# First forward gate of the Mamba block stored raw and passed through silu between the directions

## The reference

```python
x = x + _L0_conv_ref(_gn(x), Wq, Wk, Wv)       # attention, 102 highest scores of 1024 kept per row
t = _to_tokens(x)
t = t + _L1_attn_ref(_ln_t(t), ...)            # Mamba in both directions
t = t + _L1_ffn_ref(_ln_t(t), ...)             # 8 experts, top 2
...
def _mamba(x, in_proj_w, conv_w, conv_b, x_proj_w, dt_proj_w, dt_proj_b, A_log, Dvec, out_proj_w):
    xz = x @ in_proj_w.T
    xs, z = jnp.split(xz, 2, axis=-1)
    ...
    xs = jax.nn.silu(xs)
    dbc = xs @ x_proj_w.T
    dt = jax.nn.softplus(dbc[..., :DT_RANK] @ dt_proj_w.T + dt_proj_b)
    ...
    _, hs = jax.lax.associative_scan(combine, (dA, dBu), axis=1)
    y = jnp.einsum('blds,bls->bld', hs, Cm) + xs * Dvec
    y = y * jax.nn.silu(z)
    return y @ out_proj_w.T
```

## Time and profile before

| | us |
|---|---|
| median of 3 runs | 1493.72 |
| the runs | 1494.01, 1493.72, 1484.97 |
| the profiled execution, its own time | 1495.54 |
| its span, first to last instruction | 1493.7 |
| TensorE busy | 1262.7 (85%) |
| VectorE busy | 1200.8 (80%) |
| ScalarE busy | 898.4 (60%) |
| GpSimd busy | 836.4 (56%) |
| mean granted TensorE clock | 0.937 |

### The profile page before, as it was taken

One profiled execution on the slowest core, in us unless ns is written; L12 is line 12 of the kernel. 1 busy time (PEld: TensorE's weight loads), 2 busy tenths in 40 slices (PEclk: granted clock), 3 DMA queues, 4 the chain that ended last, 5 costly groups with the idle time before them and its releaser, 6 DMA issues. The chain is left out here.

```text
span 1493.7 us, 17449 instructions
## 1 busy us (share of the span) xinstructions
PE 1262.7 (85%) x4573; PEld 641.1 (43%) x4573; DVE 1200.8 (80%) x1388; ACT 898.4 (60%) x1247; POOL 836.4 (56%) x450
## 2 busy tenths in 40 slices
PE   3609888898998988988888989889898998888868
PEld 1307344344546434433444634434354733434343
DVE  2695799998796689999688679999779479999920
ACT  1626766766555766767464676676574676676612
POOL 3022388788152378778235258878517238878815
PEclk8859899999989889999999979999999988999979
DMA  2000112222030112222021012222103011322203
GB/s 77 14 0 2 46 71 84 85 92 77 16 113 15 31 57 86 85 86 97 17 77 66 4 58 79 91 85 86 56 1 114 16 37 65 98 85 84 85 1 127
DMA packets 30506, 92.00 MB, mean 62 GB/s; under 512 B 4790, under 2 KB 8764, under 8 KB 30428
## 3 DMA queue, kind: packets, MB, share of 16 engines
q1 hardware_dynamic: 30428, 91.10, 18.0%
HBM read 88.34 MB, written 2.75 MB: 61 GB/s over the span
## 5 line engine op out<-in xcount | busy, mean ns | idle before, releaser
L664 POOL TENSOR_TENSOR work<-expo,ring 128x1024 f32<-128x1024 f32 x128 | 300.1, 2365 | 164.4 <-DVE expo L1364 162.3
L664 POOL TENSOR_TENSOR ring<-ring 128x1024 f32<-128x1024 f32 x128 | 300.2, 2367 | 26.7 <-DVE ring L1364 26.7
L1364 DVE TENSOR_TENSOR_SCAN ring<-ring,ps 128x1024 f32<-128x1024 f32 x128 | 284.7, 2263 | 6.9 <-PE ps L1786 6.9
L1364 DVE TENSOR_TENSOR_SCAN expo<-ring,ps 128x1024 f32<-128x1024 f32 x128 | 285.6, 2270 | 0.0
L1822 PE MATMUL ps<-ring,ident 128*128 128x512 f32 x512 | 260.4, 615 | 25.5 <-POOL ring L664 18.7
L1822 PE MATMUL ps<-work,ident 128*128 128x512 f32 x512 | 241.1, 593 | 0.0
L953 ACT ACTIVATE ring<-dt_f,decay 128x1024 f32<-128x1024 f32 x128 | 147.0, 1148 | 118.9 <-DVE expo L1364 80.7
L719 ACT ACTIVATE b_dtx_tok<-dtx_tok,b_tok 128x256 f32<-128x256 f32 x448 | 189.2, 493 | 0.0
L1786 PE MATMUL ps<-ident,b_dtx_tok 128*128 128x128 f32 x896 | 121.8, 279 | 43.9 <-DVE expo L1364 40.1
L1786 PEld LDWEIGHTS ps<-ident,b_dtx_tok 128*128 128x128 f32 x896 | 96.8, 141 | 134.0 <-issue 69.2
L1822 PEld LDWEIGHTS ps<-ring,ident 128*128 128x128 f32 x512 | 83.7, 189 | 159.7 <-POOL ring L664 116.6
(11 more groups left out here) (280 smaller groups left out, 2075.6 us busy)
## 6 DMA issues: line engine op xcount, KB each, us to landing
ring<-c_rows SPq DMA_DIRECT2D x128, 512.0 KB, 3.6
b_dtx_tok<-comb_rows SPq DMA_DIRECT2D x16, 512.0 KB, 4.0
dtx_tok<-comb_rows SPq DMA_DIRECT2D x16, 512.0 KB, 4.7
x_c<-in_x SPq DMA_DIRECT2D x4, 512.0 KB, 3.3
out<-xs_f SPq DMA_DIRECT2D x4, 512.0 KB, 2.6
w<-in_L_ffn_w SPq DMA_DIRECT2D x2, 512.0 KB
ring<-in_L_attn_f_in_proj_w SPq DMA_DIRECT2D x1, 256.0 KB
ring<-in_L_attn_b_in_proj_w SPq DMA_DIRECT2D x1, 256.0 KB
```

Of the source, the lines that this page charges most:

```text
L664: pool.tensor_tensor(hc[odd][:, k, :], hs[odd][:, k, :], c_all[:, odd, :], ALU.mult).then_inc(hc_ready, 1)
L1364: v.tensor_tensor_scan(hs[odd][:, k, order], dA[:, k, order], dbu[:, order], 0.0, ALU.mult, ALU.add).then_inc(scan_ready, 1)
```

## The change

The first forward gate is no longer made by silu out of PSUM. It is copied raw like the others, `z_gate` is gone, and `open_gates` applies silu to four gates. In `prepare`, the copy of that gate and the copy of the B rows now stand behind the first `dt_log`, and the table load directly behind the last silu of the convolutions. `apply_gate(0,0)` waits on `gate_open` like the others.

```diff
-            def z_gate(b):
-                z_free(b, 0, 0)
-                nc.scalar.activation(gate[:, 0, 0, :], z_ps[0][0][:, :], ACT.Silu).then_inc(z_copied, 1)
-
@@ open_gates
-                for d, k in ((0, 1), (1, 0), (1, 1)):
+                for d, k in ((0, 0), (0, 1), (1, 0), (1, 1)):
                     nc.scalar.activation(gate[:, d, k, :], gate[:, d, k, :], ACT.Silu).then_inc(gate_open, 1)
@@ prepare
                 conv_silu(b, 1, 1)
-                z_gate(b)
-                b_rows(b, 0)
 
                 nc.scalar.preload_act_table_set("natural_log_exp_and_others")
                 dt_log(b, 0, 0)
+                z_copy(b, 0, 0)
+                b_rows(b, 0)
                 dt_log(b, 0, 1)
                 z_copy(b, 0, 1)
@@ apply_gate
-                if d or k:
-                    dve.wait_ge(gate_open, 3 * b + 2 * d + k)
-                else:
-                    dve.wait_ge(z_copied, 4 * b + 1)
+                dve.wait_ge(gate_open, g + 1)
```

## The result

| | before | after |
|---|---|---|
| median of 11 runs, us | 1493.72 | 1501.49 |
| range of the runs, us | 1484.97 to 1495.56 | 1497.34 to 1505.4 |
| profiled execution, us (span) | 1495.54 (1493.7) | 1502.12 (1500.3) |
| ScalarE busy, us | 898.4 | 901.7 |
| mean granted TensorE clock | 0.937 | 0.937 |

The change makes the kernel slower by 0.61%: ratio 1.0061, 95% interval 1.0044 to 1.0078, which is 9.1 us (6.6 to 11.6). The ratio is not the quotient of the two medians, which are only 7.8 us apart; the quotient of the two means is 1.0062. The forecast was 5.5 us slower, and "within 1%".

A forecast was written before the change was run, and what follows sets the result against it. VectorE bounds the states; at the entry the engines wait in turn, and TensorE's chain to the spread ends last. First exp 0, late z projections 5.5, turn 0: 5.5 us slower, 1493.72 to 1499.2 us; range 1489 to 1507.

The forecast's parts named there:

- The first exp gains nothing from the early load: 0.: Entry, ScalarE: 1.19 us leave the queue ahead of the first exp, but it waits for VectorE's cap; gain 0.
- the drain: ScalarE table switch: the skill's 1.38 us besides the 1.28 us load, by which the early load would gain.
- The B-row copy ends 4.7 us behind the first cap, and TensorE starts 2.5, 1.3, 2.9 and 1.3 us late.: Entry, TensorE: project_z(0,1) waits for the moved copy, with transposes and spread behind it; 8.0 us of late start together.
- D/2 in three images, D in one: 5.5 us.: Entry, TensorE: late start D arrives halved if the clock's rise stays put (images 0, 1, 3), whole in image 2.
- 3.2 us or more: Entry, TensorE: z matmuls ran this long before the clock's rise in all four images; evidence against the full clock.
- VectorE's chain is behind TensorE's: nothing more.: Entry, image 0: VectorE's chain ends about 170.7, the late spread about 172.3, so ScalarE's added 1.1 us costs nothing.
- The turn: 0.: Turn between table loads: a fourth silu of about 0.98 us is covered by waits; cost 0.
- the lasting low clock: Rival, entry: TensorE's hole delays the rise, all eight z records run at 1.2 GHz; plus 11.9 us, 1505.6; chance 0.20.
- The full clock: Rival, entry: the late z projections fall behind the clock's rise; 1.8 us less than before, 1491.9; chance 0.15.
- the late ScalarE: Rival, entry: ScalarE was late after all, first exp 1.19 us sooner per image; 4.8 us faster, 1488.9; chance 0.05.
- the uncovered silu: Rival, turn: the fourth silu isn't covered and adds 3.9 us to the 5.5; 1503.1; chance 0.06.

The follow-up runs named there:

- copies back: Changed kernel with the first raw gate copy and the B-row copy put back ahead of the table load, four silus kept; 1491.42 us, ratio to before 0.9999.
- B rows first: Changed kernel with only the B-row copy moved ahead of the first time step, the raw gate copy staying behind it; 1490.46 us, ratio to before 1.0001.
- the two kernels with the same entry: The kernels copies back and B rows first, whose z records start as early as in the kernel before; 1491.42 and 1490.46 us.
- the six kernels of the table: Before, changed, copies back, B rows first, gate first, and the changed kernel with both copies behind both time steps (1510.08 us, ratio to before 1.0126).
- filled hole: Changed kernel with one 512-column matmul of unused result in TensorE's hole ahead of project_z(0,1)'s wait for the B-row copy; 1500.12 us, ratio to before 1.0060.
- gate first: Changed kernel with only the raw gate copy moved ahead of the table load, the B-row copy staying behind the first time step; 1497.08 us, ratio to before 1.0043.

## Why the prediction was right or wrong

Right in sign, in "within 1%" and in the chain that carries the loss; the size was low, because one term was mis-sized. By its steps:

- *The first exp gains nothing from the early load: 0.* Right. Its idle time grew to 1.29 us, and the kernel with the copies back (late load) and the one with the B rows first (early load) are both at 1.000. The forecast had the drain of "ScalarE: Activation LUTs", section "What ACT_TABLE_LOAD costs", in the Trainium skill as what speaks for a gain; the trace disagrees again, as in the kernel with the B rows first the copy behind the load starts at 158.84 where the load from 157.55 ends at 158.83.
- *The B-row copy ends 4.7 us behind the first cap, and TensorE starts 2.5, 1.3, 2.9 and 1.3 us late.* Right in images 0 to 2: 4.59 or 4.60 us in every image, holes of 2.43, 1.22, 2.92 and 2.92 us. Image 3 had the short hole in the forecast and the long one in the trace, because the clock fell later there and the time-step projections were over sooner. The mean of the late start over the kernels with the same entry is 2.0 us an image, 8.1 in all, and the forecast had 8.0.
- *D/2 in three images, D in one: 5.5 us.* This is the term that was mis-sized: the late start was halved, and the runs show that it arrives whole. In the one pair of traces it comes near, 1.26, 1.08, 3.43 and 0.75 against 1.25, 0.65, 2.9 and 0.65, and that was luck: in the trace of the kernel before the clock rose 5.7, 5.5, 3.2 and 5.1 us behind the first z record (4.9 in the mean), in the two kernels with the same entry only 4.0 and 3.6 us in the mean, in the changed kernel 4.2 us. Over the 24 entries of the six kernels of the table it rose 2.9 to 6.1 us behind the first z record, at late starts of 0 to 5.1 us alike. So the rise moved with the start, and its place within that spread differed between executions whose work on TensorE is the same. The z records take the same 5.5 to 6.0 us in the mean, and the late start arrives whole: 8.1 us, against 9.1 (6.6 to 11.6) measured. The mistake was to take the rise of one trace as fixed. The forecast's "3.2 us or more" of z matmuls ahead of a rise tells what that one trace had; in image 1 of the kernel with the filled hole the clock rose 1.0 us behind the first z record, with the filler's records 1.9 us ahead of it.
- *VectorE's chain is behind TensorE's: nothing more.* Right; the second exp is late in the kernel with the B rows first, and its time is that of before.
- *The turn: 0.* Right, 11.59 us both times in image 0, and within 0.01 us in the others.

Two of its sums are off. The term of image 3 in the lasting low clock is 7.0 + 1.3 - 6.1 = 2.2 and not 2.0, so that end is about 12.2 us. And by its own figures the kernel breaks even when about 7 of the 8 z records run at the full clock, not 5: with 5 of them it would still be 3.3 us slower. Neither changes the forecast; the second made the full clock look likelier than it was.

Of the rivals, the late ScalarE is refuted by the B rows first (the load is early and the time is that of before), and the uncovered silu by the copies back. The full clock (1491.9) didn't come. The low clock through all eight records would have made them 7.0 us long; they took 5.2 to 6.1 in the changed kernel. Its price of 11.9 us came nearer to the measured one than the forecast's, but for another reason. The rule behind it, in the Trainium skill's "TensorE: Matmul & The Clock Gate", section "What's actually happening", says that the clock goes by how busy the engine was recently. The filled hole tests what the rival made of it: its 5.06 us against 5.60 lean that way, mostly by one image of four, and don't settle it.

## What to carry to other kernels

When an edit moves a short copy that empties a shared PSUM tile, ask which engine waits on that copy and what stands behind the wait: 0.27 us of ScalarE's time cost 9 us here, because the first spread of every image stood behind it on TensorE. A cheap instruction that releases another engine belongs in the idle time ahead of a long wait. A gain or loss that hangs on where the clock happens to rise in one trace should be counted by its mean over positions, not by the one seen. And when two traces are compared, look at the stretches that the edit doesn't touch too: here one of them took 1.5 us more in the images in which a stretch at the low clock lasted longer.

## What the runs showed of the hardware

- The two levels of the clock move the time of the same eight z records, to the start of the next matmul, between 3.95 us (filled hole) and 6.54 us (gate first). The kernel before and the two whose z records start as early as in it (copies back, B rows first) took between 1482 and 1497 us, the fastest at a mean granted clock of 0.949 and the slowest at 0.937. The moments of fall and rise differ from image to image and from execution to execution.
- The stretch at 0.50 behind the first products lasted 10.2 us in 32 of 48 images, 13.7 us in 15 and 6.8 us in one, in kernels with the same work there, and VectorE reached its first gate product 1.5 us later with the stretch of 13.7 us than with that of 10.2 us.
- Matmuls on 128 rows between two projections on 16 rows didn't hold the clock up: four records took 3.77 us behind them, 0.9 us each, where z records at the full clock start 0.43 us apart (155.58, 156.01, 156.44 us in the kernel before).
- A switch of ScalarE's tables took the 1.28 us of the load and at most 0.03 us more: in the kernel with the B rows first 1.31 us lie between the end of the silu (157.53) and the start of the copy (158.84). At the turn of the kernel before, the load from 275.49 ends at 276.77 and the first silu starts at 276.78.
